# Cross attentions of a four-layer network: summed softmax denominators written once, reciprocals spread by transfers, outputs copied by ScalarE, maxima in bf16 parts

## The reference

```
x = x + tanh(g_xattn[l]) * xattn_l(layernorm(x), ctx)
x = x + tanh(g_ffn[l])   * ffn_l(layernorm(x))

def xattn(x, ctx):                    # layers 0, 1, 3
    q, k, v = heads(x @ Wq + bq), heads(ctx @ Wk + bk), heads(ctx @ Wv + bv)
    scores = einsum('bhqd,bhkd->bhqk', q, k) * scale     # layer 0: q, k rotated
    attn = softmax(scores, axis=-1)
    return merge(einsum('bhqk,bhkd->bhqd', attn, v)) @ Wo + bo
```

## Time and profile before

| | us |
|---|---|
| median of 3 runs (2495.61 to 2498.07) | 2497.26 |
| profiled execution | 2511.05 |
| its span, first to last instruction | 2509.1 |
| stage L0_xattn, 0 to 235.3 | 235.3, PE busy 197.07 |
| stage L1_xattn, 979.4 to 1183.0 | 203.6, PE busy 177.35 |
| stage L3_xattn, 1680 to 1909 | 229.0, PE busy 191.55 |

### The profile page before, as it was taken

How to read it: one execution, slowest core, us unless ns; L and a number is a source line. 1 busy time by engine, 2 the same in 40 slices (tenths; PEclk the granted TensorE clock), 3 DMA queues, 4 the chain that set the end, 5 groups by cost and what they waited for, 6 DMA issues and landing times.

```text
span 2509.1 us, 40654 instructions
## 1 busy us (share of the span) xinstructions
PE 2340.0 (93%) x15494; PEld 1663.0 (66%) x15494; DVE 1409.9 (56%) x2881; ACT 958.3 (38%) x2302; POOL 613.3 (24%) x548
## 2 busy tenths in 40 slices
PE   6997999999999998898999999988984999999998
PEld 4444677776666665444666765544543999999997
DVE  7886654774445455887466533348875444444442
ACT  1366655444545553332233322124643222222222
POOL 3234222252001002211233200024455122222222
PEclk8999999999999999999999999989996999999999
DMA  5011201121001000100001039502126222222221
GB/s 201 1 35 57 68 17 43 35 89 47 26 26 51 26 26 26 70 1 17 1 1 36 1 99 322 181 0 110 42 71 240 66 35 35 35 35 37 36 37 26
DMA packets 73767, 144.70 MB, mean 58 GB/s; under 512 B 11592, under 2 KB 62536, under 8 KB 71120
## 3 DMA queue, kind: packets, MB, share of 16 engines
q1 hardware_dynamic: 41280, 100.94, 11.9%
q0 software_dynamic: 16368, 26.23, 5.4%
q10 hardware_dynamic: 15936, 15.03, 2.2%
HBM read 107.42 MB, written 71.09 MB: 71 GB/s over the span
## 4 chain that ended last, share of the span: by engine, by line
PE 80%; DVE 11%; ACT 3%; issue 3%; POOL 2%; DMA 1%; another core or an unknown queue 1%; SPq 0%; DVEq 0%; POOLq 0%; ACTq 0%
PE PS L2366 14%; PE PS L2392 7%; PE PS L2801 5%; PE PS L2813 4%; PE PS L1540 4%; PE PS L1531 4%; PE PS L2050 3%; PE PS L2062 3%; PE PS L2870 3%; PE PS L2835 3%; PE PS L602 3%; PE PS L2861 3%; DVE mem L1143 3%; DVE mem L1148 2%; PE PS L2906 2%
## 5 line engine op out<-in xcount | busy, mean ns | idle before, releaser
L2366 PEld LDWEIGHTS PS<-ctx2T,x_all 128*128 128x128 f32 x3124 | 361.2, 193 | 10.0 <-DVE x_all L2515 6.4
L2366 PE MATMUL PS<-ctx2T,x_all 128*128 128x128 f32 x3124 | 361.8, 276 | 5.8 <-DVE x_all L2515 5.0
L2563 POOL DMA_INDIRECT out_x<-xnT,moe_small x71 | 130.8, 1842 | 428.4 <-ACT xnT L2448 425.4
L2392 PE MATMUL PS<-mem,moe_small 128*128 x852 | 195.8, 379 | 0.8 <-ACT xnT L2448 0.8
L2515 DVE COPY x_all<-mem 128x2816 f32 x71 | 115.5, 1627 | 110.1 <-issue 96.9
L2392 PEld LDWEIGHTS PS<-mem,moe_small 128*128 128x128 f32 x852 | 156.4, 190 | 19.5 <-issue 1.2
L1148 DVE RECIPROCAL mem<-PS 128x512 f32<-128x512 f32 x48 | 160.8, 3350 | 10.4 <-PE PS L671 10.2
L1143 DVE TENSOR_REDUCE mem<-PS 128x32 f32<-128x2048 f32 x48 | 109.8, 2288 | 55.3 <-PE PS L627 51.1
L3190 DVE TENSOR_REDUCE moe_small<-PS 128x2 f32<-128x1024 f32 x64 | 78.4, 1225 | 102.0 <-PE PS L2861 100.1
L3335 POOL TENSOR_TENSOR mem<-mem,moe_small 128x512 f32<-128x512 f32 x64 | 82.2, 1304 | 207.7 <-DVE moe_small L3200 207.7
L2801 PE MATMUL PS<-xnT,mem 128*128 128x512 f32 x256 | 127.0, 618 | 0.8 <-ACT xnT L2987 0.8
(11 more groups left out here) (378 smaller groups left out, 4519.6 us busy)
## 6 DMA issues: line engine op xcount, KB each, us to landing
slots<-in_trash_rows SPq DMA_DIRECT2D x8, 4290.0 KB, 64.3
mem<-in_L_ffn_experts SPq DMA_DIRECT2D x8, 2176.0 KB, 11.6
xn<-unit_rows SPq DMA_DIRECT2D x15, 512.0 KB, 3.8
xn<-slots ACTq DMA_DIRECT2D x53, 130.0 KB, 2.1
x_all<-in_x SPq DMA_DIRECT2D x8, 512.0 KB, 8.2
mem<-unit_rows SPq DMA_DIRECT2D x8, 512.0 KB
out_x<-x_all ACTq DMA_DIRECT2D x8, 512.0 KB
unit_rows<-moe_small SPq DMA_DIRECT2D x7, 512.0 KB, 3.2
```

The costliest lines, as they stand in the source:

```text
L2366: last = nc.tensor.matmul(PS[:, moe_bank(j, part), c * P:(c + 1) * P], m.w[:, j % 2, k, at:at + P], m.rowT[:, j % 2, k, :], start=k == 0, ...
L2392: last = nc.tensor.matmul(PS[:, MOE_BANK_Y, 0:D], m.hT[:, j % 2, n, :], w[:, :, at:at + D], start=n == 0, stop=n == KE - 1)
L2563: nc.gpsimd.indirect_dma_start(s.T["out"], bass.IndirectOffsetOnAxis(s.token[:, j % 4:j % 4 + 1], 0), m.result[:, j % 4, :], None, compute ...
```

## The change

Five things change in the three cross attentions.

**Maxima.** After both halves of the maxima, DVE splits the f32 values into three bf16 parts (`split_max`: copy, subtract, copy, subtract). PE turns the parts in bf16, and one bf16 matmul with a table that adds the three parts takes the place of the f32 one. The copy of the turned maxima has two buffers.

**Denominators.** For all but the last half batch of a stage, four tables `sums_of_tile` place the sums of query tile t in row t of each head, so that 128x128 numbers hold what 128x512 held. PE does this in 16 matmuls of 128 columns where there were 4 of 512.

**Reciprocals.** DVE takes the reciprocal of the 128x128 tile; SP stores it to memory and loads it back spread to 128x512 (`spread_recips`), one half batch at a time through one buffer.

**Outputs.** ACT copies values from PSUM (`copy_o`), and DVE multiplies them in SBUF, one place later in its order than before. PE's next values wait for ACT's copy.

**Order.** The first part of the projection moves behind the transposes of the maxima in L1 and L3. Weight loads of the stage after L1_xattn and L3_xattn are issued by ACT in turn 2 or 1. POOL folds a scale later in turns 0 and 1.

```diff
+def split_max(eng, order, s, b):
+    eng.wait_ge(s.sems["max_ready"], 2 * (b + 1))
+    order.mark(eng.tensor_copy(max_part(s, 0), s.max))
+    order.settle()
+    order.mark(eng.tensor_tensor(s.max_rest, s.max, max_part(s, 0), ALU.subtract))
+    order.settle()
+    order.mark(eng.tensor_copy(max_part(s, 1), s.max_rest))
+    order.settle()
+    eng.tensor_tensor(max_part(s, 2), s.max_rest, max_part(s, 1), ALU.subtract).then_inc(s.sems["max_split"], 1)
+def spread_recips(sp, s, b, f):
+    k = KD * b + f
+    few = s.recips[f].rearrange("(q r) n -> q r n", r=HD)[:, 0:TB, :].rearrange("q t n -> q (t n)").rearrange("q (o n) -> q o n", o=1)
+    sp.wait_ge(s.sems["recip_ready"], k + 1)
+    sp.dma_start(s.recips[f], s.recip_few).then_inc(s.sems["recip_stored"], 16)
+    sp.wait_ge(s.sems["recip_stored"], 16 * (k + 1))
+    wait_for(sp, s.sems["o_ready"], k)
+    sp.dma_start(s.recip, few.broadcast_to([NH // KD, HD, S])).then_inc(s.sems["recip_spread"], 16)
...
     def turn_max(b):
-        pe.wait_ge(s.sems["max_ready"], 2 * (b + 1))
+        pe.wait_ge(s.sems["max_split"], b + 1)
...
-            last = nc.tensor.matmul(PS[:, g, :], s.minus_max[r, f, :], s.maxT[r, :], start=False, stop=True)
+            last = nc.tensor.matmul(PS[:, g, :], s.minus_max[r, f, :], s.maxT[r, b % 2, :], start=False, stop=True)
...
-        wait_for(pe, s.sems["o_ready"], KD * b + f)
+        wait_for(pe, s.sems["o_copied"], KD * b + f)
...
-        for c in range(G):
-            last = nc.tensor.matmul(PS[c * GR:(c + 1) * GR, BANK_DEN, :], s.sums, s.probsT[:, f, c, :], start=True, stop=True)
+        if (b, f) == (B - 1, KD - 1):
+            for c in range(G):
+                last = nc.tensor.matmul(PS[c * GR:(c + 1) * GR, BANK_DEN, :], s.sums, s.probsT[:, f, c, :], start=True, stop=True)
+        else:
+            for t in range(TB):
+                for c in range(G):
+                    last = nc.tensor.matmul(PS[c * GR:(c + 1) * GR, BANK_DEN, 0:P], s.sums_of_tile[:, t, :],
+                                            s.probsT[:, f, c, t * P:(t + 1) * P], start=t == 0, stop=t == TB - 1)
...
 def units_sync(sp, e, s):
     u = s.units
-    for b in range(EARLY_UNITS):
+    for n in range(1, EARLY_UNITS + 4):
+        if 0 <= n - 2 < B - 1:
+            spread_recips(sp, s, n - 2, 1)
+        if n - 1 < B:
+            spread_recips(sp, s, n - 1, 0)
+        b = n - 4
+        if b < 0:
+            continue
...
+    def copy_o(b, f):
+        act.wait_ge(s.sems["pv_psum"], KD * b + f + 1)
+        wait_for(act, s.sems["y_psum"], 2 * (b - 1))
+        nc.scalar.activation(s.o[:, b % 2, f, :], PS[:, BANK_O, :], ACT.Copy).then_inc(s.sems["o_copied"], 1)
...
+        if s.act_loads and n == (1 if handed else 2):
+            act.wait_ge(e.x_updated, s.x_before)
+            for dst, src in s.next.loads:
+                act.dma_start(dst, src).then_inc(s.next.weights_loaded, 16)
...
     def normalise(b, f):
-        dve.wait_ge(s.sems["den_psum"], KD * b + f + 1)
-        dve.reciprocal(s.recip, PS[:, BANK_DEN, :]).then_inc(s.sems["recip_ready"], 1)
-        dve.wait_ge(s.sems["pv_psum"], KD * b + f + 1)
-        dve.wait_ge(s.sems["recip_ready"], KD * b + f + 1)
-        dve.tensor_tensor(s.o[:, b % 2, f, :], PS[:, BANK_O, :], s.recip, ALU.mult).then_inc(s.sems["o_ready"], 1)
+        dve.wait_ge(s.sems["o_copied"], KD * b + f + 1)
+        if (b, f) == (B - 1, KD - 1):
+            dve.wait_ge(s.sems["recip_ready"], KD * b + f + 1)
+        else:
+            dve.wait_ge(s.sems["recip_spread"], 16 * (KD * b + f + 1))
+        o = s.o[:, b % 2, f, :]
+        dve.tensor_tensor(o, o, s.recip, ALU.mult).then_inc(s.sems["o_ready"], 1)
```

More of the change, by code:

```diff
@@ L53, in shape_constants @@
         out[name] = ((row[:, None] // HD) == half[None, :]).astype(f) * f(scale)
-    out["minus_max"] = np.concatenate([-(row[:, None] == (2 * k + p // SC)[None, :]).astype(f) for k in range(KD)], 1)
+    of_part = (row < 4 * PARTS)[:, None] & (row[:, None] % 4 == (np.arange(KD)[:, None] * 2 + (p // SC)[None, :]).reshape(1, -1))
+    out["minus_max"] = bf16_pairs(-of_part.astype(f))
     out["sums"] = ((p // SC)[:, None] == (np.arange(GR) // HD)[None, :]).astype(f)
+    place = np.arange(GR) % HD
+    of_tile = (place[None, :] == np.arange(TB)[:, None]) | ((place >= TB)[None, :] & (np.arange(TB) == 0)[:, None])
+    out["sums_of_tile"] = (out["sums"][:, None, :] * of_tile[None, :, :]).astype(f).reshape(P, TB * GR)
     swap = np.zeros((P, P), f)
@@ L83 @@
 ROTARY = ("cos_q", "sin_q", "cos_k", "sin_k")
-OF_A_STAGE = ROTARY + ("earlier", "of_head8", "of_head4", "minus_max", "sums")
+OF_A_STAGE = ROTARY + ("earlier", "of_head8", "of_head4", "minus_max", "sums", "sums_of_tile")
 def constant_columns():
@@ L381, in _ @@
                         sp.dma_start(dst, src).then_inc(later.keys_loaded, 16)
-                    for dst, src in later.loads:
+                    for dst, src in later.loads if not s.act_loads else ():
                         sp.dma_start(dst, src).then_inc(later.weights_loaded, 16)
@@ L563, in logits_bank, with max_part, recips_sync @@
     return 2 if b >= B - 2 else BANK_M
+def max_part(s, part):
+    n = 2 * KD * TB
+    return s.max_parts.rearrange("p (g n) -> p g n", g=G)[:, :, part * n:(part + 1) * n]
+def split_max(eng, order, s, b):
[15 more added lines that the diff above has]
+    sp.dma_start(s.recip, few.broadcast_to([NH // KD, HD, S])).then_inc(s.sems["recip_spread"], 16)
+def recips_sync(sp, e, s):
+    for b in range(B):
+        for f in range(KD):
+            if (b, f) != (B - 1, KD - 1):
+                spread_recips(sp, s, b, f)
 def xattn_pe(pe, e, s):
@@ L775, in xattn_pe @@
                 turn_y(n - 3)
-            if old and not s.front:
-                project_out(n - 2, 0)
         if before:
@@ L783, in xattn_pe @@
             logits(n - 3)
-        if old and s.front:
-            project_out(n - 2, 0)
         if now:
@@ L995, in xattn_act @@
         now, before, old, route, place = turn_of(s, n)
+        if old:
+            copy_o(n - 2, 1)
         if n + 1 < B:
@@ L1031, in xattn_act @@
     if m:
+        copy_o(B - 1, 1)
         normalised(B - 2)
@@ L1276, in xattn_dve @@
             norm_stats(n - 3)
+        if old and n - 2 == B - 1:
+            normalise(n - 2, 0)
         if old:
-            normalise(n - 2, 1)
+            reciprocals(n - 2, 1)
+        if old and n - 2 < B - 1:
+            normalise(n - 2, 0)
         if route:
@@ L1284, in xattn_dve @@
             maxima(n, 1)
+            if n == 0:
+                dve.wait_ge(s.sems["zeroed"], 1)
+            split_max(dve, order, s, n)
+        if old:
+            normalise(n - 2, 1)
         if early and n == 4:
```

67 lines of the change are left out of this document (44 added, 23 removed).

## The result

| | us |
|---|---|
| before, median of 4 runs | 2497.44 (2495.61 to 2498.07) |
| after, median of 4 runs | 2514.9 (2512.27 to 2516.52) |
| ratio after/before, 95% interval | 1.0064 (1.0050 to 1.0078) |
| after, profiled execution | 2516.52, span 2514.6 |

The change makes the kernel 17.5 us slower, where 20 us faster were forecast and 2452 to 2492 us given as range. Run a second time beside other kernels it gave 1.0061 (1.0045 to 1.0078).

What follows compares the result with a forecast made beforehand. PE, with 80% of the chain, was taken as the bound. L0 -12.7, its unit rows +22.9, L1 -12.9 and L3 -17.2 sum to -19.9 us: 2491.1 profiled, scaled to 2477 us; range 2452 to 2492.

Steps and rivals of the forecast that it cites:

- the steady turns: Middle turns of each stage: L0 1.3 us shorter, L1 1.65 us, L3 1.4 us, to near 20.8, 18.6 and 20.3 us.
- PE's wait for the bank in L0: Second half of an L0 turn: splitting and multiplication stand ahead of the rotation on DVE, so PE waits some 1.3 us.
- the keys: Matmuls adding the turned maxima: bf16 in place of f32 saves 0.73 us a set, 48 times.
- the short reciprocals: On DVE: reciprocal falls from 3.35 to about 0.9 us, 47 times, seen by PE only where it waited.
- A round trip in quiet: Store and spread of one reciprocal through memory: 5.2 us, bounds 4.4 and 10; hidden by 3.8 us in a normal turn.
- the store of unit rows: L0: this store stands behind both spreads in SP's queue, delaying ACT's sums of products and then PE: +22.9 us.
- The waits that I put down as 4.35 and 5.0 us: L0: PE waits 4.35 us for queries in turns 5 and 6, and 5.0 us for exponentials in turns 7 and 8.
- Rival (a): L0: the unit store does not hold ACT, so the 22.9 us do not come; 2454 us, chance 0.20.
- rival (c): Short sums on PE: column-group loads do not overlap four ways, +1.0 us a set, 47 times; 2523 us, chance 0.08.
- Moved loads and POOL's new order: Next stage's weight loads issued by ACT and POOL's later scale: no further cost, weights of L1_ffn being read two turns later.
- Rival (b): Round trips exceed 5.2 us because transfers share 16 engines with other traffic: 2483 to 2497, middle 2490 us; chance 0.22.
- the ends of the stages: Last turns: L0's 7 to 9 -3.2 us; L1's 7 -2.3, 8 -1.6, last projection -0.7; L3's 7 -2.5, 8 -5.3, end +0.4.

Runs made afterwards that it cites:

- The second execution: The kernel before, unchanged, measured and profiled once more: ratio 0.9998, profiled execution 2502.22 us, span 2500.3 us.

## Why the prediction was wrong, step by step

**Right, within 0.4 us:** the steady turns. Forecast 20.8, 18.65 and 20.3 us, measured 20.51, 18.67 and 20.2 to 20.37. PE's wait for the bank in L0 was forecast at 1.3 us and is 1.27. In such turns the keys, the splitting and the short reciprocals cost about what the rows said (0.65 us saved a set of keys, against 0.73; a reciprocal of 128 columns 0.95 us, against 0.9). A round trip in quiet took 5.5 us (reciprocal ready 1173.3, multiplication 1178.82) against 5.2.

**Right:** the store of unit rows, +22.9 us forecast, 23.1 measured by taking it away, or 25.1 counted from turn 5 on. The waits that I put down as 4.35 and 5.0 us are 6.30 and 5.26 us in turns 5 and 6 and 7.25 and 8.78 us in 7 and 8; part of these is there without the stall (2.06 us each in 7 and 8). Against the run with the store moved, turns 5 and 6 are 7.8 and 6.4 us longer (6.1 each forecast), and turns 7 to 9 together 11.0 (10.7). Rival (a) is out.

**Right:** rival (c) did not come. From first matmul to the next line a set of short sums takes 0.98 us (for example 1783.19 to 1784.17 in L3); I had 1.1 to 1.2. The Trainium skill (TensorEngine Tiling (Array Packing), Restrictions) says that column tiling disables fast weight load; the trace shows no cost of that in this form.

**Wrong, 14.3 us: "Moved loads and POOL's new order: nothing more, since the weights of L1_ffn are first read two turns later."** I asked who reads the loads and not what travels beside them. L1's turn 2 was forecast 0.25 us longer and is 5.6 longer; L3's 3.5 us shorter, with 2.0 us set aside for shared engines, and is 5.5 longer. Rival (b) had the mechanism, "because 64 KB and 256 KB share 16 engines with weight loads", but spread it evenly as trips of 8 to 10 us; they are 5.5 us nearly everywhere and 16.0 us (1053.4 to 1069.4) and 13.5 us (1749.3 to 1762.9) once in each stage. In L1 the runs show this cause: 20.28 us without transfers, 19.87 with the loads spread. In L3 they show it for some 6 of the 9 us missed there (29.95 to 23.77 us). The other 2.6, from the 21.2 us forecast to 23.77, came with no wait for a transfer: DVE works off the statistics of three batches in a row in that turn, and the first cast takes 1.84 us, where I had put 0.25 for each operation of the splitting. How much each of these holds is not shown.

**Wrong, about 13 us: the ends of the stages.** L0's turns 7 to 9 were to be 3.2 us shorter; without the unit-row stall they are 3.6 us longer, and L1's last wait grew by 4.8 us where I had written -0.7. In a steady turn a spread has 3.8 us of slack because a turn lies behind it. At the end no turn does: spread, multiplication, full reciprocal and second multiplication stand in a row in one buffer. This is read from the rows; the run with a second buffer bears it out for 3.15 us in L0 and 1.2 us in L3, not in L1, and not in the total. I used the steady turn's reading for turns that are not steady.

**Wrong, some 7 us in small parts of both signs.** The largest: L1's turns 1 and 7, 2.4 and 2.8 us longer than forecast; 2.3 us in L0_ffn, where I counted none; L3's turns 0 and 1, 1.4 us, as the transposes of the maxima in turn 0 wait for DVE 4.72 us where they waited 2.21; the first cast of the splitting takes 1.64 us there.

**The base.** The forecast's sum was scaled from a profiled execution that was 0.55% above the median. The second execution shows that the excess sat in places, 6.5 us of it in L3's turns 5 to 7 and 3.8 us in L1's turns 0 and 7, and not everywhere. It did little to the sum, since the steps used steady turns, but a scale factor does not describe it.

Together 14.3 + 13 + 7 = 34 us, the distance between the forecast's -19.9 and the traces' +14.3. The direction failed because the gain, 1.6 us a turn in some 15 turns, was set against one stall only, while transfers on the path brought more of them in the turns that are not steady: beside the loads, and at the ends.

## To carry to other kernels

When a step goes through memory, list every other transfer that can be in flight in each turn, not only its own queue and its own readers; a latency of 5.5 us became 16 us beside 4.3 MB of weights. Read first, last and loading turns by themselves: slack in the steady turn says nothing about them. And try the parts of a change together and apart: here bf16 maxima lost 0.5% with full reciprocals and won 0.4% on top of the short reciprocals, which had freed the engine that they load.
